# VectorE instead of GpSimd scales the softmax weights, and products, angle tiles, value projections and the opening's transposes change their places

## The chip, the cores and the metric

One core of one Trainium2 chip runs the whole layer. The metric is the device time of one execution in microseconds; lower is better. A group of runs is summed up by its median.

## The reference, cut to what matters

Four sequences of 512 tokens with 128 features pass an adaptive-layernorm block: an attention with 16 query heads, 4 key/value heads and 4 "nodes" per head, and a mixture of experts. The change lies in the attention alone:

```python
q, k, v = (x @ wq), (x @ wk), (x @ wv)              # heads of 64
logits = x @ wr                                     # 4 nodes for each token and head
tk_vals, tk_idx = top_k(logits, 2); tk_w = softmax(tk_vals)
pos = cumsum(member) - member                       # a token's place in each node's list
for n in range(4):
    c, s = cos_c[pos[..., n]], sin_c[pos[..., n]]   # rotary angles by that place
    qr = q * c + rotate_half(q) * s;  kr = k * c + rotate_half(k) * s
    scores = where(causal & member_of_n, qr @ kr.T * SCALE, NEG)
    outs[n] = softmax(scores) @ v
y = sum over the two chosen nodes of tk_w * outs[node]
x = x + gate * (y @ wo)                             # then the experts
```

## The kernel before

Each engine has its own instruction stream, written out in order; semaphores tie the streams together. After an opening (layernorm, ranking of the nodes, positions, the first rotary tables) one loop runs over k = 4n + s: n is one of 64 heads (4 sequences of 16), s one of 4 query tiles of 128 tokens, which sees (s+1)*128 keys. Each step works on two scores, one for each chosen node (e = 0, 1). After the loop come the experts, which the change leaves alone.

**A step, by engine.** TensorE (PE): `scores(k)`; `flip(k+2)`, the transposes of rotated q and k of a later step; `prob_rows(k-4)`, the transposes of weighted probabilities; in odd heads at s = 2 `values` (L1597), in heads with n % 4 = 2 at s = 2 `project_value`, in heads with n % 8 = 4 the output projection; at s = 3 `project(n+3)`. ScalarE (ACT): the copy of the flipped tile (`QK`, L740), the copy of the transposed probabilities (L751), `weigh_a(k-2)` (L772), which scales the first score's probabilities by its coefficient, then `exponentials(k)` (L763). VectorE (DVE): `row_max(k)` (L1147, L1157), `keep_angles` (L1069, L1071), `weigh_b(k-3)` (L1168, two inputs in SBUF beside the scalar), `inverse_sums(k-1)` (the reciprocal L1163), masks of the next head at s = 3 (L1141), `size_angles` (L1075), `products` (L1088). GpSimd (POOL): `rotate` in four parts for the head two ahead (L532 twice, L537, L540, L544, L548, L551), a split of expert weights at s = 1 of heads 2 to 49 (L571, L573), a split of later sequences' rows at s = 3 of heads 4 to 15 (L490, L492), and `coefficients(k-1)` (L560): `coef = rden * wslot` on 128x2.

**What sets the order.** A coefficient waits for its reciprocal; `weigh_a` and `weigh_b` wait for it. `rotate(m, 0)` waits for all four products of head m, which DVE makes in head m-2: two at s = 0 and two at s = 1. The last part of `rotate(m)` counts `k_done` up, and `flip(4m)`, which stands in PE's stream at s = 2 of head m-1 ahead of `values`, waits for it.

**PSUM.** Bank 7 (`psM`) holds in turn a head's projection, read by the products, the values, the value projection and the output projection. Banks 4 to 6 are a ring of turns (`turns`, `turn_bank`, `wait_turn`): flips, probability transposes and angle tiles take the next bank each, in PE's order, and wait for the reader of the turn three before. Banks 0 to 3 hold scores.

**Angle tiles.** Rotary tables are made for spans of 8 heads. The next span's four tiles stand in four heads one after the other (n % 8 = 0 to 3); at n % 8 = 4 ACT loads the sine table, makes sine and cosine of the span (L714, L715) and loads the exponential's table again (L808, L810).

**The opening.** `position_rows(b)` for the four sequences all use bank 4, so each waits for ACT's copy of the one before (`keep_positions`, L706); three of the four `chosen_rows` use bank 0 in the same way (L700). ACT loads the exponential's table (L726) ahead of those copies. The first flip waits for all four copies of positions and for the first head's rotation, which DVE makes (last line L1125).

## Time and profile before

| | us |
|---|---|
| median of 3 runs (918.26 to 919.42) | 919.1 |
| the profiled execution | 918.83 |
| its span, first to last instruction | 917.1 |
| loop, from the first to the last head's first score matmul | 58.87 to 783.8 |
| 8 heads in the middle (24 to 31) | 92.35 |

PE is busy 90% of the span, DVE 86%, ACT 80%, POOL 65%. The granted TensorE clock is 1.00 of full speed in the loop. From head 8 to head 55 eight heads take 92.2 to 92.6 us each time, so one such span stands for the rest. Matmuls overlap, so a busy PE is not a PE at its peak; an idle engine costs something only where the path runs through it.

### The profile page before, as it was taken

The numbers are of one execution on the slowest core, as the hardware profiler recorded it, in microseconds if no ns is written. First come the engines' busy times: TensorE is split into PE (matmuls) and PEld (weight loads), VectorE is DVE, ScalarE is ACT, GpSimd is POOL, SyncE is SP. The second block draws the span as 40 slices with busy tenths as digits, with TensorE's granted clock in tenths as the row PEclk, the third lists the DMA queues.
The fourth block names the chain that finished last, engine by engine and source line by source line (L and its number), as shares of the span: only waits on it lengthen the run. The fifth ranks groups of instructions, "written<-read, shape, count | busy, mean of one in ns | idle before, by whom it ended". The sixth has DMA issues, their size and how long they took to land. (4 is left out here: it accounts for less than half of the span.)

```text
span 917.1 us, 21368 instructions
## 1 busy us (share of the span) xinstructions
PE 826.5 (90%) x6552; PEld 580.4 (63%) x6552; DVE 792.9 (86%) x2003; ACT 733.0 (80%) x2001; POOL 600.4 (65%) x944
## 2 busy tenths in 40 slices
PE   4478989999999999999999999999999999999893
PEld 4456656666666666666666666666666666575793
DVE  6889978998899889988998899889988888777894
ACT  7268898889888988898889888988888887865572
POOL 4527768777877677767776777677656666127492
PEclk9699999999999999999999999999999999999997
DMA  9111111111211111111121111121101110323553
GB/s 219 32 18 30 37 31 43 37 36 25 43 41 37 24 41 39 38 29 37 36 41 30 39 37 36 32 41 31 14 9 16 16 14 13 127 70 93 153 166 113
DMA packets 81039, 45.01 MB, mean 49 GB/s; under 512 B 35072, under 2 KB 79808, under 8 KB 80928
## 3 DMA queue, kind: packets, MB, share of 16 engines
q1 hardware_dynamic: 79712, 41.15, 20.2%
q0 software_dynamic: 1216, 2.51, 0.8%
q8 instruction: 55, 0.90, 0.4%
q14 instruction: 56, 0.46, 0.2%
HBM read 30.62 MB, written 12.43 MB: 47 GB/s over the span
## 5 line engine op out<-in xcount | busy, mean ns | idle before, releaser
L1573 PE MATMUL psum<-QK 128*128 128x128 f32 (+3 forms) x1024 | 367.5, 451 | 2.3 <-ACT QK L740 1.8
L763 ACT ACTIVATE probs<-psum,negmax 128x128 f32<-128x128 f32 (+3 forms) x512 | 266.2, 527 | 48.6 <-DVE negmax L1157 32.5
L532 POOL TENSOR_TENSOR R<-pcs 128x512 f32<-128x512 f32 x126 | 172.7, 1392 | 59.7 <-DVE pcs L1088 59.7
L1573 PEld LDWEIGHTS psum<-QK 128*128 128x128 f32 x1024 | 158.3, 191 | 48.0 <-issue 41.8
L1168 DVE SCALAR_TENSOR_TENSOR accs<-probs,coef,accs 128x128 f32<-128x128 f32 (+3 forms) x256 | 164.7, 643 | 2.5 <-ACT accs L772 2.5
L772 ACT ACTIVATE accs<-probs,coef 128x128 f32<-128x128 f32 (+3 forms) x256 | 147.7, 577 | 23.4 <-POOL coef L560 23.2
L1088 DVE TENSOR_TENSOR pcs<-psum,arena 128x512 f32<-128x512 f32 x256 | 162.1, 674 | 1.7 <-POOL R L532 1.3
L560 POOL TENSOR_TENSOR coef<-rden,wslot 128x2 f32<-128x2 f32 x256 | 53.0, 207 | 167.9 <-DVE rden L1163 167.9
L1586 PE MATMUL psum<-ident,accs 128*128 128x128 f32 x640 | 115.9, 279 | 25.8 <-ACT QK L740 20.0
L1157 DVE CUSTOM_DVE_ANT_0 psum<-psum,outside 128x512 f32<-128x512 f32 x128 | 87.7, 700 | 51.4 <-PE psum L1575 50.7
L740 ACT ACTIVATE QK<-psum 128x384 f32<-128x384 f32 x235 | 115.6, 492 | 0.0
L1558 PE MATMUL psum<-ident,R 128*128 128x128 f32 x512 | 99.9, 277 | 11.0 <-issue 9.2
L751 ACT ACTIVATE arena<-psum 128x384 f32<-128x384 f32 (+1 forms) x242 | 107.0, 443 | 0.0
L1586 PEld LDWEIGHTS psum<-ident,accs 128*128 128x128 f32 x640 | 72.8, 140 | 51.2 <-issue 27.5
L1577 PE MATMUL psum<-mring 128*128 128x128 f16 (+2 forms) x384 | 104.8, 273 | 0.0
L763 ACT ACTIVATION_READ_ACCUMULATOR probs<-psum,negmax 128x1 f32 x512 | 103.1, 201 | 0.0
L1558 PEld LDWEIGHTS psum<-ident,R 128*128 128x128 f32 x512 | 56.6, 142 | 57.8 <-issue 51.4
L1147 DVE TENSOR_REDUCE negmax<-psum 128x2 f32<-128x256 f32 (+1 forms) x128 | 70.3, 550 | 18.9 <-PE psum L1577 18.0
L1575 PE MATMUL psum<-causal,identbig 128*128 128x128 f16 x384 | 84.3, 219 | 0.0
L1597 PE MATMUL psum<-arena,v_b 128*64 128x256 f32 (+3 forms) x512 | 76.0, 439 | 0.7 <-ACT arena L751 0.7
L1560 PE MATMUL psum<-ident,ktoks 128*128 128x128 f32 x256 | 69.9, 273 | 0.0
L1157 DVE CUSTOM_DVE_ANT_0 psum<-psum,causal 128x384 f32<-128x384 f32 x128 | 68.4, 573 | 0.6 <-PE psum L1577 0.6
(278 smaller groups left out, 1560.9 us busy)
## 6 DMA issues: line engine op xcount, KB each, us to landing
weight_halves<-whl SPq DMA_DIRECT2D x48, 128.0 KB, 2.2
arena<-weight_halves SPq DMA_DIRECT2D x22, 256.0 KB, 3.1
wrow<-words SPq DMA_DIRECT2D x64, 86.0 KB
arena<-weight_halves SPq DMA_DIRECT2D x7, 512.0 KB, 6.8
wrow<-words SPq DMA_DIRECT2D x64, 42.0 KB
wst<-in_L_ffn_w_up_dram SPq DMA_DIRECT2D x14, 128.0 KB, 2.4
wst<-in_L_ffn_w_gate_dram SPq DMA_DIRECT2D x14, 128.0 KB, 2.4
wst<-in_L_ffn_w_down_dram SPq DMA_DIRECT2D x14, 128.0 KB, 2.4
```

The lines of the kernel that those rows point to most:

```text
L532: pool.tensor_tensor(R[u][:, :, :, 0:3:2, half * HALF:(half + 1) * HALF].rearrange("p t e j f -> p (t e) j f"), halves(pc, half), halves(p ...
L740: act.activation(QK[:, n % 2, :, tb * P:(tb + 1) * P], turn_bank(("t", i))[:, 0:3 * P].rearrange("p (j t) -> p j t", j=3), ACT.Copy, scale ...
L751: act.activation(accT[:, n % 3, 0:w, ib * P:(ib + 1) * P], turn_bank(("pt", k))[:, 0:w * P].rearrange("p (j i) -> p j i", j=w), ACT.Copy). ...
L763: act.activation((expB if e else expA)[:, k % (4 if e else 3), 0:w], area, ACT.Exp, scale=1.0 if k % TB < 2 else -1.0, bias=negmax[k % 4][ ...
L772: act.activation(acc[k % 4][:, 0:w], expA[:, k % 3, 0:w], ACT.Copy, scale=coef[k % 4][:, 0:1]).then_inc(S["wa_done"], 1)
L1088: dve.tensor_tensor(dst[:, :, e, :].rearrange("p t (j f) -> p t j f", f=HALF), src, table.unsqueeze(2).to_broadcast([P, TB, 4, HALF]), ALU ...
L1157: dve.tensor_tensor_reduce(score_area(k, e), score_area(k, e), outside[:, e, 0:w].bitcast(BF16) if s == TB - 1 else causal[:, T - w:T], -1 ...
L1168: dve.scalar_tensor_tensor(acc[k % 4][:, 0:w], expB[:, k % 4, 0:w], coef[k % 4][:, 1:2], acc[k % 4][:, 0:w], ALU.mult, ALU.add).then_inc(S ...
L1558: pe.transpose(psT[:, e * P:(e + 1) * P], R[u][:, tb, e, 0:2, :].rearrange("p c d -> p (c d)"), ident[:, :])
L1573: pe.matmul(o, QK[:, u, e, rows], QK[:, u, 2, 0:w], start=True, stop=False)
L1577: mm_ = pe.matmul(o, mring[:, r, 1 + e, rows], mring[:, r, 0, 0:w], start=False, stop=True)
L1586: mm_ = pe.transpose(psPT[:, jb * P:(jb + 1) * P], acc[k % 4][:, jb * P:(jb + 1) * P], ident[:, :])
```

## The change

- `coefficients(k-1)` moves from POOL's stream to the end of DVE's step k, behind that step's products.
- The four products of head n+2 are no longer made as 2, 2, 0, 0 over the steps of head n: where n is even and n % 8 is not 4 they are made as 1, 2, 1, 0 (head 0 has an order of its own).
- Angle tiles 0 to 3 stay in heads 0 to 3; the others stand in odd heads from 5 to 51, one in each. `keep_angles` waits for the products that still read the table it overwrites.
- `project_value` goes to a turn bank, a new kind "v" in the ring, and waits for its turn instead of for the products. `project` no longer waits for `keep_value`.
- In the opening `position_rows` use banks 4, 4, 6, 5 and `chosen_rows` banks 0 to 3, with waits for the angles' readers; the table load of the exponential moves behind the first `keep_qk`; the second projection moves behind the transposes; one multiplication of the mixing weights (`dif * L`) moves from DVE to POOL.

```diff
 def angle_tile(k):
     n, s = k // TB, k % TB
-    if s == 1 and n % SPAN < TB and n // SPAN + 1 < NH // SPAN:
-        return n // SPAN * TB + n % SPAN
-    return None
+    if s != 1 or n >= (NH // SPAN - 2) * SPAN + TB:
+        return None
+    if n < TB:
+        return n
+    return n // SPAN * TB + (n % SPAN - 1) // 2 + 2 if n % 2 and n >= SPAN - 3 else None
+
+def products_at(k):
+    n, s = k // TB, k % TB
+    if n + 2 >= NH:
+        return ()
+    if n == 0:
+        return (((1, 2), (1, 3)), (), [(2, which) for which in range(4)], ())[s]
+    spread = n % 2 == 0 and n % SPAN != TB
+    of = (((0,), (1, 2), (3,), ()) if spread else ((0, 1), (2, 3), (), ()))[s]
+    return [(n + 2, which) for which in of]
...
+    if k % TB == 2 and k // TB % GROUP == 2 and k // TB // GROUP + 1 < B * KV:
+        turns.append(("v", k // TB // GROUP + 1))
...
 # GpSimd
-def coefficients(k):
...
+pool.wait_ge(S["lg_ev"], 2)
+pool.wait_ge(S["w_step"], 1)
+pool.tensor_tensor(dif, dif, L, ALU.mult).then_inc(S["w_step"], 1)
...
     if m < NH:
         rotate(m, part)
-    if k >= 1:
-        coefficients(k - 1)
 # ScalarE
 trigonometry(0)
-act.preload_act_table(ACT.Exp)
 keep_chosen(0, 0)
-keep_positions(1)
 keep_chosen(1, 0)
-keep_positions(2)
+for b in range(1, B):
+    keep_positions(b)
 keep_chosen(0, 1)
-keep_positions(3)
 keep_chosen(1, 1)
...
 keep_qk(0)
+act.preload_act_table(ACT.Exp)
 # VectorE
-dve.tensor_tensor(dif, dif, L, ALU.mult).then_inc(S["w_step"], 1)
...
+    if a >= TB:
+        dve.wait_ge(S["prod_done"], 4 * SPAN * (a // TB))
...
+def coefficients(k):
+    n, s = k // TB, k % TB
+    a = (n // H * TB + s) * H + n % H
+    if k == 0:
+        dve.wait_ge(S["w_done"], 2)
+    dve.wait_ge(S["rden_done"], k + 1)
+    dve.tensor_tensor(coef[k % 4][:, :], rden[k % 4][:, :], wslot[:, a, :], ALU.mult).then_inc(S["coef_done"], 1)
...
-    if k == 0:
-        products(1, 1)
-    elif n == 0 and s < 3:
-        products(2, s - 1)
-    elif s < 2 and n + 2 < NH:
-        products(n + 2, s)
+    for m, which in products_at(k):
+        product(m, which)
+    if 1 <= k <= STEPS:
+        coefficients(k - 1)
 # TensorE
 def position_rows(b):
     if b:
-        pe.wait_ge(S["row_ev"], b)
-    dst = bank[4]
+        pe.wait_ge(S["row_ev"], 1)
+    if b == 2:
+        pe.wait_ge(S["trig_done"], TB)
+        pe.wait_ge(S["ang_abs"], TB)
+    if b == 3:
+        pe.wait_ge(S["words_done"], 1)
+    dst = position_bank(b)                 # bank[(4, 4, 6, 5)[b]]
...
     if s == 2 and n % GROUP == 2 and n // GROUP + 1 < B * KV:
-        pe.wait_ge(S["prod_done"], 4 * (n + 3))
+        wait_turn(pe, ("v", n // GROUP + 1))
         project_value(n // GROUP + 1)
...
-        pe.wait_ge(S["v_ev"], min(B * KV, (n + 2) // GROUP + 1))
```

## Rows read from the trace of the kernel before

**Rows 1.** The page, part 1: busy time, share of the span, instructions.

```profile
PE 826.5 (90%) x6552; PEld 580.4 (63%) x6552; DVE 792.9 (86%) x2003; ACT 733.0 (80%) x2001; POOL 600.4 (65%) x944
```

**Rows 2.** Stretches of two heads, 24 to 31: length; busy by engine; clock; DMA.

```profile
339.08:361.66 22.58, 21.44 (x147) 14.08 (x145) 21.48 (x55) 18.84 (x58) 16.22 (x27) 1.00 0.18 37
361.66:384.25 22.59, 21.65 (x160) 14.50 (x157) 21.21 (x55) 19.12 (x59) 16.22 (x27) 1.00 0.18 37
384.25:409.82 25.57, 24.22 (x175) 17.20 (x173) 21.71 (x56) 23.11 (x57) 16.82 (x27) 1.00 0.17 33
409.82:431.43 21.61, 20.95 (x156) 14.15 (x153) 18.64 (x49) 18.92 (x59) 17.02 (x27) 1.00 0.19 39
```

**Rows 3.** The waits: engine, line, who released it; total, times, longest.

```profile
POOL coef L560 <- DVE rden L1163: 167.9, 156, 4.3
...
ACT accs L772 <- POOL coef L560: 23.2, 26, 4.5
```

**Rows 4.** Groups of DVE by line and shape: busy, mean ns, idle before.

```profile
L1088 DVE TENSOR_TENSOR pcs<-psum,arena 128x512 f32<-128x512 f32 x256 | 162.1, 674 | 1.7 <-POOL R L532 1.3 <-ACT arena L715 0.4
...
L1168 DVE SCALAR_TENSOR_TENSOR accs<-probs,coef,accs 128x128 f32<-128x128 f32 x64 | 32.5, 508 | 0.0
```

**Rows 5.** Timeline of DVE, heads 29 to 31: start, length, what, idle before.

```profile
409.20 0.35 DVE L1168 SCALAR_TENSOR_TENSOR accs<-probs,coef,accs 128x128 f32<-128x128 f32 x1
...
417.19 0.15 DVE L1163 RECIPROCAL rden<-den 128x2 f32<-128x2 f32 x1
...
418.69 1.01 DVE L1168 SCALAR_TENSOR_TENSOR accs<-probs,coef,accs 128x128 f32<-128x128 f32 x1
...
429.21 0.70 DVE L1157 CUSTOM_DVE_ANT_0 psum<-psum,outside 128x512 f32<-128x512 f32 x1 [2.09 <-PE psum L1575]
```

**Rows 6.** Timeline of POOL, heads 30 and 31.

```profile
415.45 2.94 POOL L532 TENSOR_TENSOR R<-pcs 128x512 f32<-128x512 f32 x2 [0.59 <-DVE pcs L1088]
...
418.51 1.04 POOL L537 TENSOR_TENSOR R<-R,code 128x512 f32<-128x512 f32 x1
...
421.46 0.19 POOL L560 TENSOR_TENSOR coef<-rden,wslot 128x2 f32<-128x2 f32 x1 [0.44 <-DVE rden L1163]
...
423.40 1.08 POOL L551 TENSOR_TENSOR ktoks<-R,kwork 128x256 f32<-128x256 f32 x1
```

**Rows 7.** Timeline of PE: the flip before head 31's values, head 32's first score.

```profile
424.94 0.38 PE L1558 MATMUL psum<-ident,R 128*128 128x128 f32 x2
...
431.43 0.44 PE L1573 MATMUL psum<-QK 128*128 128x128 f32 x2
```

**Rows 8.** Timeline of DVE in the opening: the first head's last rotation line.

```profile
55.92 0.42 DVE L1125 TENSOR_TENSOR ktoks<-R,kwork 128x256 f32<-128x256 f32 x1
```

**Rows 9.** Timeline of PE: the first flip; head 1's second score.

```profile
57.74 0.44 PE L1558 MATMUL psum<-ident,R 128*128 128x128 f32 x2 [0.24 <-ACT posT L706]
...
74.89 0.70 PE L1573 MATMUL psum<-QK 128*128 128x256 f32 x2 [1.37 <-ACT QK L740]
```

**Rows 10.** Timeline of ACT: table load, first exponential, the first two weighings.

```profile
49.51 1.28 ACT L726 ACT_TABLE_LOAD   x1
...
60.43 0.37 ACT L763 ACTIVATE probs<-psum,negmax 128x128 f32<-128x128 f32 x1 [1.22 <-DVE negmax L1147]
...
68.68 0.40 ACT L772 ACTIVATE accs<-probs,coef 128x128 f32<-128x128 f32 x1 [4.53 <-POOL coef L560]
...
72.62 0.51 ACT L772 ACTIVATE accs<-probs,coef 128x256 f32<-128x256 f32 x1 [2.04 <-POOL coef L560]
```

**Rows 11.** Timeline of POOL: head 1's rotation, with nothing between its parts.

```profile
61.73 2.50 POOL L532 TENSOR_TENSOR R<-pcs 128x512 f32<-128x512 f32 x2 [16.87 <-DVE pcs L1088]
...
67.58 0.72 POOL L551 TENSOR_TENSOR ktoks<-R,kwork 128x256 f32<-128x256 f32 x1
```

**Rows 12.** Stretches of two heads, 6 and 7, and 58 and 59.

```profile
132.22:154.02 21.80, 20.95 (x155) 14.15 (x153) 18.41 (x49) 19.01 (x59) 18.29 (x31) 1.00 0.19 39
...
729.91:751.47 21.56, 20.88 (x155) 14.22 (x153) 18.54 (x49) 18.91 (x59) 14.49 (x23) 1.00 0.11 15
```

More of the change, by code:

```diff
@@ L312, in turn_bank, with position_bank, value_bank @@
             return bank[4 + turn_of[what] % 3]
+        def position_bank(b):
+            return bank[(4, 4, 6, 5)[b]]
+        def value_bank(g):
+            return turn_bank(("v", g)) if g else psM
         def wait_turn(eng, what):
@@ L573, in split @@
                 pool.tensor_tensor(whl[:, 1, :], wst[:, :], whl[:, 0, :], ALU.subtract).then_inc(S["w_lo"], 1)
-            for k in range(STEPS + 1):
+            for k in range(STEPS):
                 n, s = k // TB, k % TB
@@ L700, in keep_chosen @@
                 act.activation(mk[0:HD, half * 2:half * 2 + 2, 1 + e, :],
-                               bank16[(0, 0, 5, 0)[e + 2 * half]][0:HD, 0:2 * NEAR].rearrange("p (b t) -> p b t", b=2), ACT.Copy,
+                               bank16[e + 2 * half][0:HD, 0:2 * NEAR].rearrange("p (b t) -> p b t", b=2), ACT.Copy,
                                scale=BIG).then_inc(S["mk_ev"], 1)
@@ L705, in keep_positions @@
                 act.wait_ge(S["row_mm"], b + 1)
-                act.activation(posT[0:PIECED, b * T:(b + 1) * T], bank[4][0:PIECED, :], ACT.Copy, scale=1.0 / TURN
+                act.activation(posT[0:PIECED, b * T:(b + 1) * T], position_bank(b)[0:PIECED, :], ACT.Copy, scale=1.0 / TURN
                                ).then_inc(S["row_ev"], 1)
@@ L1077, in size_angles, with product @@
                                   ).then_inc(S["ang_abs"], 1)
-            def products(n, e):
-                dve.wait_ge(S["qk_mm"], n + 1)
-                dve.wait_ge(S["trig_done"], TB + 1 + 2 * (n // SPAN))
-                if n >= 1 and e == 0:
-                    dve.wait_ge(S["add_done"], 2 * n)
-                src = psM.rearrange("p (t j f) -> p t j f", t=TB, f=HALF)
-                for i, dst in ((1, pc), (0, ps)):
-                    table = trig[:, n // SPAN % 2, i, n % SPAN, :, e, :]
-                    dve.tensor_tensor(dst[:, :, e, :].rearrange("p t (j f) -> p t j f", f=HALF), src,
-                                      table.unsqueeze(2).to_broadcast([P, TB, 4, HALF]), ALU.mult
-                                      ).then_inc(S["prod_done"], 1)
+            def product(n, which):
+                e, (i, dst) = which // 2, ((1, pc), (0, ps))[which % 2]
+                if which == 0:
+                    dve.wait_ge(S["qk_mm"], n + 1)
+                    dve.wait_ge(S["trig_done"], TB + 1 + 2 * (n // SPAN))
+                    if n >= 1:
+                        dve.wait_ge(S["add_done"], 2 * n)
+                src = psM.rearrange("p (t j f) -> p t j f", t=TB, f=HALF)
+                table = trig[:, n // SPAN % 2, i, n % SPAN, :, e, :]
+                dve.tensor_tensor(dst[:, :, e, :].rearrange("p t (j f) -> p t j f", f=HALF), src,
+                                  table.unsqueeze(2).to_broadcast([P, TB, 4, HALF]), ALU.mult
+                                  ).then_inc(S["prod_done"], 1)
             def first_rotation():
@@ L1100, in over_slot @@
                     return t_.unsqueeze(2).to_broadcast([P, TB, HD])
-                for e in range(2):
-                    products(0, e)
+                for which in range(4):
+                    product(0, which)
                 dve.wait_ge(S["code_e"], 2)
@@ L1129, in _ @@
             dve.tensor_reduce(lmax[:, 0, :], dif, AX_X, ALU.add).then_inc(S["w_step"], 1)
-            products(1, 0)
+            for which in range(2):
+                product(1, which)
             dve.tensor_scalar(shift[:, :, :, :].rearrange("p b h s -> p b (h s)"),
@@ L1438, in project_value @@
                 for tb in range(TB):
-                    mm_ = three(psM[:, tb * HD:(tb + 1) * HD], rows_of(b, tb),
+                    mm_ = three(value_bank(g)[:, tb * HD:(tb + 1) * HD], rows_of(b, tb),
                                 [w_v[:, l, (g % KV) * HD:(g % KV + 1) * HD] for l in range(2)], True, True)
@@ L1473, in chosen_rows @@
                 pe.wait_ge(S["sel_cp"], e + 1)
-                if half and not e:
-                    pe.wait_ge(S["words_done"], 1)
-                else:
-                    pe.wait_ge(S["mk_ev"], 4 + e + half)
+                pe.wait_ge(S["mk_ev"], 4)
+                if e + half:
+                    pe.wait_ge(S["trig_done"], TB)
+                    pe.wait_ge(S["ang_abs"], TB)
                 for t_ in range(B // 2 * (TB - 1)):
                     tile = (half * B // 2 + t_ // (TB - 1)) * TB + t_ % (TB - 1)
-                    mm_ = pe.transpose(bank16[(0, 0, 5, 0)[e + 2 * half]][0:HD, t_ * P:(t_ + 1) * P], sel16[:, e, tile * 64:(tile + 1) * 64],
+                    mm_ = pe.transpose(bank16[e + 2 * half][0:HD, t_ * P:(t_ + 1) * P], sel16[:, e, tile * 64:(tile + 1) * 64],
                                        ident16[:, :])
```

22 lines of the change are left out of this document (8 added, 14 removed).

## The prediction

> **What bounds the kernel now.** I read the page's busy shares first [rows 1], then the stretches of two heads in the loop [rows 2], then the waits [rows 3], then the timelines. No engine is full over the whole span, but in the loop the two heads 24/25 and 26/27, which hold two angle tiles each, have DVE busy for 21.48 of 22.58 us and 21.21 of 22.59: 95% and 94% [rows 2]. There DVE sets the pace. The pair 30/31 has no tile, takes 21.61 us, and DVE works 18.64 of it; it waits 2.09 us for scores behind the values [rows 2, 5]. The pair 28/29 takes 25.57 because of the tables and the output projection [rows 2]. So eight heads cost 92.35 us, and DVE is busy 83.04 of them, about 90%. POOL's 167.9 us of waiting for reciprocals [rows 3] is idle time of an engine that does not bind; ACT's 23.2 us of waiting for coefficients [rows 3] can matter.
>
> **Part 1, the coefficients go to DVE.** The sum needs the price of a DVE operation on 128x2 with two inputs in SBUF, which the trace lacks. The nearest row is the reciprocal on 128x2, 0.15 us long, whose successor starts about 0.08 after it [rows 5]: 0.1 us of DVE's line, my estimate, times 256. But there is more. `weigh_b` on 128x128 takes 0.35 us when POOL is idle; at 418.69 it took 1.01, while POOL's L537 ran from 418.51 to 419.55 [rows 5, 6]. It ended 0.15 us behind POOL's instruction, as if it had waited for it and then run. Over all 64 of that shape the mean is 508 ns [rows 4], 0.16 more than the free one. It goes both ways: two L532 that a `weigh_b` comes between take 2.94 us, two that ran free 2.50 [rows 6, 11]. A coefficient also reads two SBUF tensors, and POOL is busy 66.28 of 92.35 us [rows 2]. I take 0.15 us of waiting per coefficient, by the 508 ns row; the bounds are 0 and 0.66 (1.01 less 0.35).
>
> The Trainium skill states a rule that speaks against this part: page "SBUF — State Buffer", section "Who interferes with whom", says that a VectorE instruction with two SBUF inputs and a GpSimd instruction that reads SBUF exclude each other, and whoever issues second blocks until the first is done. The rows just named agree. By that rule, if coefficients mostly arrive second, the time would be near the slow rival's 943 us; without it near the fast rival's 912, both worked out below from rows.
>
> In eight heads DVE gets 32 coefficients: 3.2 us of work and 4.8 of waiting, 83.0 to 86.2 or 91.0. At the 95% that the busiest pair reaches, eight heads then need 90.7 or 95.8 us, against 92.35. So this part alone allows anything from a gain of 1.7 to a loss of 3.4 in each span, and the detail decides.
>
> **Part 2, products 1, 2, 1 and angle tiles in odd heads.** Moving a tile costs no work. With two tiles a pair has 2.6 to 2.8 us more DVE work than without [rows 2], some 1.4 each, and the 2.09 us of waiting in an odd head [rows 5] hides one. That is the gain: the two angle pairs lose a tile in their even head. The pair 30/31, and 28/29, gain a tile instead.
>
> The price lies in POOL. In head 30 POOL starts the rotation at 415.45, as the second pair of products ends, and ends it at 424.48 (423.40 + 1.08): 9.03 us [rows 6]. PE's flip of that head starts at 424.94, 0.46 later, at once behind its scores [rows 7]. Now the fourth product follows the third reciprocal (417.19) instead: 417.19 + 0.08 + 0.67 [rows 5, 4] is 417.9, less 0.3 that a lighter first step saves (my estimate): 417.6, against 415.4. POOL's 9.03 us shrink: three coefficients leave it (0.19 each) and the 0.44 us wait for a reciprocal [rows 6]: 8.0, and I take 8.1, with one of DVE's coefficients in between. If both L532 run free, as at 61.73 [rows 11], 7.7; if DVE's coefficients come between its parts as `weigh_b` does, 8.6. So the rotation ends at 417.6 + 0.1 + 8.1 = 425.8, and the flip, which could start at 424.6, waits for it. Behind that flip stand in PE's stream the probability transposes, `values`, the next scores and the next head: from the flip to head 32's first score PE needs 6.49 us [rows 7] without a pause. The pair therefore takes 21.61 + 425.8 - 424.94 = 22.5 us (22.1 by 7.7, 23.0 by 8.6). The three pairs of a span that are spread have the same structure afterwards, so all three get 22.5, against 22.58, 22.59 and 21.61: +0.7 in a span, +0.24 a pair.
>
> - Spread pairs among heads 16 to 49: 13, +3.1 us.
> - Heads 6 to 15 also split rows on POOL, 18.29 us a pair against 17.02 [rows 12, 2], some 0.6 a head in the same chain: 23.0 for four pairs, two of which stood at 21.8 [rows 12] and two near 22.6: +3.1. Head 2 keeps its tile and spreads too, so its fourth product comes 1.4 us later still: +0.9, an estimate.
> - Pairs with tables, seven: the step before the sine tables stays 2, 2, 0, 0 and gets two coefficients of 0.25 us ahead of ACT's chain; I take +0.4 each, +2.8 (0 to +1).
> - After head 49 POOL has no weight split and the chain is a microsecond shorter, so flips do not wait: four pairs, one of which loses its even tile, three at 21.56 [rows 12]: -1.0 in all.
>
> **Part 3, values in a turn bank.** It lets the value projection run before the spread product; its turn's reader, ACT's copy, is done by then. The next flips find their bank a turn later. I cost it at nothing, covered by PE's score matmuls of s = 3; if uncovered, about 0.15 us in 15 heads, inside the range.
>
> **Part 4, the opening.** The first flip starts at 57.74, released by ACT's positions copy [rows 9]; the rotation that it also needs ends at 56.34 (55.92 + 0.42) [rows 8]. With more banks the copies are early, so it gains up to 1.3 us. The table load of 1.28 us now stands before the second copy and the first exponential, which had waited 1.22 us idle [rows 10]; that hides most of it, 0.3 stays: -1.0 (bounds 0 and -1.3). Then the first two coefficients: ACT waited 4.53 and 2.04 us for them behind POOL's rotation [rows 10]. On DVE the first is ready before ACT comes; the second stands behind four products at once. Head 1's second score at 74.89, held by ACT's copy [rows 9], can come 1.7 us earlier (bounds 0 and 2.5); its rotation on POOL, 61.73 to 68.30 [rows 11], is not shortened. The multiplication that leaves DVE costs nothing either way: DVE waits for the angles behind it, and POOL, which takes it, is idle until 61.73 (16.87 us, rows 11). Sum: -2.7.
>
> **The sum.** -2.7 + 0.9 + 3.1 + 3.1 + 2.8 - 1.0 = +6.2 us on the profiled execution's 918.8 (917.1 span and 1.7 around it; the median of the runs is 0.3 higher): **925.0 us**, slower by 0.7%.
>
> **Rivals.**
> - *Faster: POOL's chain is short enough.* If coefficients slip between POOL's instructions and the chain takes 7.6 us, the flip waits for nothing that ACT's copy does not hold too, and spread pairs run at 21.9: 13 x -0.36 is -4.7, the early four +1.1, head 2 +0.3, tables +1.4, the end -1.4, the opening -3.5: -6.8, 912 us. It decides where the rotation ends less than 0.3 us behind the old flip. For it: DVE's 18.64 us in the pair 30/31 leave room, and the coefficients of even heads' first three steps meet an idle POOL. Against it: two L532 at 2.94 us and a slack of 0.46 us.
> - *Slower by much: DVE becomes the bound.* If coefficients wait for POOL as the 418.69 row did, DVE's 91.0 us per span at 95% make 95.8, spread pairs 23.1: +10.9, early four +5.9, head 2 +1.5, tables +7, the end +1, the opening -2: +24, 943 us.
> - *No change: gains and losses cancel.* Pairs at 22.26, their mean now, 0; early four +2, head 2 +0.5, tables +1.4, the end -1, the opening -2.9: 918.8. Then the spread only trades DVE's wait for POOL's.
>
> **How the numbers follow.** A measurement of this kernel can tell about 0.2%, 1.8 us. Chances: forecast 0.42, its own range 921 to 932; faster rival 0.32; no change 0.13; slow rival 0.13. So faster 0.32, same 0.13, slower 0.55. Eight in ten lie between 909 and 938: the lower end leaves the outer third of the faster rival, the upper half of the slow one.
>
> **What would show it.** Right: DVE's share in the loop rises above 93%; groups of the coefficient show a mean well over 0.15 us; PE's flip (the transposes of R) shows idle time before it in odd heads, released by POOL's last rotation line; spread pairs at about 22.5 us. ACT's long waits for coefficients in heads 0 and 1 are gone, and the first score comes near 57.9. Wrong: coefficients at 0.15 us flat, flips without idle time, or pairs below 22.0; then the first rival holds. Pairs above 23 with DVE over 96% busy speak for the second.

## The result: 941.5 us, slower by 2.5%

| | before | changed |
|---|---|---|
| median of 4 runs, us | 919.26 (918.26 to 920.74) | 941.54 (939.83 to 945.22) |
| the profiled execution, us | 918.83 | 941.49 |
| ratio, 95% interval | | 1.0246 (1.0213 to 1.0280) |

The page of the changed kernel, part 1, to be read beside [rows 1]:

```profile
PE 830.0 (88%) x6552; PEld 585.5 (62%) x6552; DVE 868.8 (92%) x2258; ACT 739.3 (79%) x2001; POOL 565.4 (60%) x689
```

The stretches of two heads, 24 to 31, and their sum, beside [rows 2]:

```profile
352.47:375.31 22.84, 21.07 (x146) 14.01 (x143) 22.80 (x60) 19.16 (x60) 15.83 (x19) 1.00 0.21 36
375.31:398.08 22.77, 20.99 (x158) 14.35 (x155) 22.73 (x60) 18.92 (x59) 15.06 (x19) 1.00 0.20 36
398.08:424.78 26.70, 24.76 (x178) 17.46 (x175) 25.52 (x67) 23.49 (x59) 15.35 (x19) 1.00 0.16 32
424.78:447.82 23.04, 21.22 (x158) 14.37 (x155) 23.00 (x60) 19.16 (x61) 15.33 (x19) 1.00 0.18 37
sum 95.35, PE 88.04 PEld 60.18 DVE 94.06 ACT 80.73 POOL 61.57; mean PE 22.01 PEld 15.05 DVE 23.52 ACT 20.18 POOL 15.39
```

The third number of work in a row is DVE's: 94.06 of 95.35 us, against 83.04 of 92.35 before. In the pairs without tables DVE has 0.04 us to spare. So eight heads cost 3.0 us more, and DVE's time grew by 11.0. The waits, beside [rows 3]:

```profile
POOL R L554 <- DVE pcs L1101: 253.3, 54, 13.5
...
ACT accs L784 <- DVE coef L1185: 52.3, 134, 2.3
...
PE psum L1583 <- POOL ktoks L573: 12.0, 9, 1.7
```

ACT waits twice as long for coefficients as before (52.3 against 23.2 us). The flips (L1583) do wait for POOL's last rotation line, as forecast, but for 12.0 us in all. The groups of DVE by shape, beside [rows 4]:

```profile
L1185 DVE TENSOR_TENSOR coef<-rden,wslot 128x2 f32<-128x2 f32 x256 | 73.4, 287 | 0.5
...
L1190 DVE SCALAR_TENSOR_TENSOR accs<-probs,coef,accs 128x128 f32<-128x128 f32 x64 | 40.0, 625 | 0.0
...
L1087 DVE TENSOR_SCALAR arena<-arena 128x512 uint32<-128x512 uint32 x28 | 29.1, 1041 | 0.0
...
L1061 DVE TENSOR_SCALAR arena<-psum 128x512 uint32<-128x512 uint32 x4 | 2.8, 692 | 1.4 <-PE psum L1555 1.4
```

The coefficient is there with 0.287 us in the mean, and `weigh_b` on 128x128 went from 508 to 625 ns. The surprise is L1087, the sign line of an angle tile (`size_angles`). Before, the same group reads:

```profile
L1075 DVE TENSOR_SCALAR arena<-arena 128x512 uint32<-128x512 uint32 x28 | 11.4, 407 | 0.0
```

Nobody touched its work, and it costs 17.7 us more. The timelines of DVE, then of POOL, in head 29 of the changed kernel show how:

```profile
421.45 0.15 DVE L1177 RECIPROCAL rden<-den 128x2 f32<-128x2 f32 x1
421.52 1.19 DVE L1087 TENSOR_SCALAR arena<-arena 128x512 uint32<-128x512 uint32 x1
422.64 0.68 DVE L1185 TENSOR_TENSOR coef<-rden,wslot 128x2 f32<-128x2 f32 x1
```

```profile
421.05 1.38 POOL L559 TENSOR_TENSOR R<-R,code 128x512 f32<-128x512 f32 x1
422.39 0.90 POOL L562 TENSOR_TENSOR kwork<-R 128x256 f32<-128x256 f32 x1
```

L559 runs until 422.43, and the sign line ends 0.28 after it; L562 runs until 423.29, and the coefficient, 0.14 us when free, ends 0.03 after it. Each DVE line stands behind a POOL line that was there first. It is so with the other sign lines: one of the 28 meets no POOL line and takes 0.41 us; the other 27 take from 0.43 to 1.42 us, 20 of them 1.19 to 1.20, and each ends 0.28 to 0.29 us behind the POOL line that had begun before it.

### The profile page after: what moved, and what is told of

Read it like the earlier page. It is cut to its first block and busy times, and to the rows that moved or that the text cites. A ratio compares the mean times of both kernels' runs of the same rounds, so it can differ in the third digit from the quotient of the medians.

```text
span 939.7 us, 21282 instructions
## 1 busy us (share of the span) xinstructions
PE 830.0 (88%) x6552; PEld 585.5 (62%) x6552; DVE 868.8 (92%) x2258; ACT 739.3 (79%) x2001; POOL 565.4 (60%) x689
## 5 line engine op out<-in xcount | busy, mean ns | idle before, releaser
L554 POOL TENSOR_TENSOR R<-pcs 128x512 f32<-128x512 f32 x126 | 165.9, 1337 | 253.6 <-DVE pcs L1101 253.3
L784 ACT ACTIVATE accs<-probs,coef 128x128 f32<-128x128 f32 (+3 forms) x256 | 145.5, 568 | 52.8 <-DVE coef L1185 52.3
L1190 DVE SCALAR_TENSOR_TENSOR accs<-probs,coef,accs 128x128 f32<-128x128 f32 (+3 forms) x256 | 174.7, 682 | 1.7 <-ACT accs L784 1.7
L1583 PE MATMUL psum<-ident,R 128*128 128x128 f32 x512 | 100.7, 279 | 23.9 <-POOL ktoks L573 12.0
L1583 PEld LDWEIGHTS psum<-ident,R 128*128 128x128 f32 x512 | 58.5, 143 | 69.3 <-issue 66.8
L559 POOL TENSOR_TENSOR R<-R,code 128x512 f32<-128x512 f32 x63 | 73.1, 1161 | 4.1
L1185 DVE TENSOR_TENSOR coef<-rden,wslot 128x2 f32<-128x2 f32 x256 | 73.4, 287 | 0.5
```

The source lines that it names most:

```text
L554: pool.tensor_tensor(R[u][:, :, :, 0:3:2, half * HALF:(half + 1) * HALF].rearrange("p t e j f -> p (t e) j f"), halves(pc, half), halves(p ...
L784: act.activation(acc[k % 4][:, 0:w], expA[:, k % 3, 0:w], ACT.Copy, scale=coef[k % 4][:, 0:1]).then_inc(S["wa_done"], 1)
L1190: dve.scalar_tensor_tensor(acc[k % 4][:, 0:w], expB[:, k % 4, 0:w], coef[k % 4][:, 1:2], acc[k % 4][:, 0:w], ALU.mult, ALU.add).then_inc(S ...
L1583: pe.transpose(psT[:, e * P:(e + 1) * P], R[u][:, tb, e, 0:2, :].rearrange("p c d -> p (c d)"), ident[:, :])
```

## The experiments

Ratios are against the kernel before, on the same chip; its median lay between 918.7 and 920.8 us on the chips used, so two times of this table can differ by some 2 us for that alone. "Eight heads" are heads 24 to 31, with DVE's busy time behind the slash.

| kernel | us | ratio (95%) | eight heads / DVE |
|---|---|---|---|
| before | 919.3 | | 92.35 / 83.04 |
| changed | 941.5 | 1.0246 (1.0213 to 1.0280) | 95.35 / 94.06 |
| 1 coefficients alone | 964.7 | 1.0491 (1.0459 to 1.0523) | 99.30 / 95.58 |
| 2 changed, coefficients back | 978.2 | 1.0632 (1.0599 to 1.0665) | 98.90 / 83.80 |
| 3 changed, tiles back | 958.2 | 1.0402 (1.0367 to 1.0437) | 97.57 / 93.24 |
| 4 opening and values alone | 930.3 | 1.0111 (1.0088 to 1.0135) | 93.37 / 82.74 |
| 5 changed, sign line late | 941.3 | 1.0232 (1.0188 to 1.0276) | 94.72 / 90.63 |
| 6 changed, scalar coefficients | 947.8 | 1.0310 (1.0265 to 1.0355) | not used |
| 7 both of 5 and 6 | 953.7 | 1.0359 (1.0322 to 1.0397) | not used |
| 8 opening alone | 921.4 | 1.0015 (0.9994 to 1.0036) | not used |
| 9 changed, split behind | 928.9 | 1.0091 (1.0057 to 1.0126) | 93.39 / 91.48 |
| 10 both of 5 and 9 | 929.6 | 1.0111 (1.0073 to 1.0150) | 93.26 / 90.62 |
| 11 as 10, coefficients early | 963.0 | 1.0461 (1.0425 to 1.0497) | not used |
| 12 opening, tiles, values | 919.4 | 0.9986 (0.9968 to 1.0004) | 91.78 / 83.94 |
| 13 changed, products two and two | 950.8 | 1.0318 (1.0270 to 1.0365) | 96.39 / 95.00 |
| 14 tiles and values alone | 918.9 | 0.9988 (0.9970 to 1.0006) | not used |
| 15 as 14, split behind | 919.0 | 0.9980 (0.9959 to 1.0000) | not used |
| 16 as 14, early heads mended | 915.8 | 0.9959 (0.9945 to 0.9974) | 91.75 / 83.91 |

### 1. The coefficients alone

```diff
 # before, POOL
-    coefficients(k - 1)
 # before, DVE, behind products
+    coefficients(k - 1)
```

> The kernel before with one change: the 256 coefficients stand on VectorE, behind the products of their step, and no longer on POOL. Opening, products (2, 2, 0, 0), angle tiles and values stay. In the changed kernel DVE is busy 94.06 of 95.35 us in heads 24 to 31, against 83.04 of 92.35 before; coefficients are 9.4 us of that, weigh_b 3.0 more, the sign line of the angle tiles 3.2 more. Theory (DVE is the bound, and the coefficients make it so): this part alone does most of the loss. DVE's work for eight heads goes to 92 to 98 us, the span of eight heads to 94 to 97, and, with no gain from the opening, the time to 932 to 945. Rival (the forecast's: the late fourth product makes POOL's rotation late and flips wait): nothing is late here, POOL loses 6.6 us of coefficients in eight heads, DVE's 3.2 us of work goes into its idle time, and the time is 916 to 923. Also open: does the sign line, 0.40 us before and 1.19 in the changed kernel, lengthen here too, where the tiles stand as before? If POOL's waits for reciprocals kept its long lines out of its way, yes (over 0.7); if it was the place in odd heads, no (0.40).

Measured: 964.7, worse than the changed kernel. Its first two pairs of the eight heads, and the sum:

```profile
350.71:375.64 24.93, 21.65 (x147) 14.05 (x145) 24.86 (x62) 18.93 (x57) 15.69 (x19) 1.00 0.16 33
375.64:400.83 25.19, 22.05 (x159) 14.52 (x157) 25.12 (x63) 19.64 (x61) 15.48 (x19) 1.00 0.16 33
...
sum 99.30, PE 89.09 PEld 60.17 DVE 95.58 ACT 81.93 POOL 61.83; mean PE 22.27 PEld 15.04 DVE 23.90 ACT 20.48 POOL 15.46
```

DVE is full in the pairs with two tiles (24.86 of 24.93), and the sign line is long here too, with the tiles where they always stood:

```profile
L1064 DVE TENSOR_SCALAR arena<-arena 128x512 uint32<-128x512 uint32 x28 | 28.9, 1033 | 0.0
```

So its length comes from the coefficients' move and not from the odd heads. The size was missed: even the theory said 945 at most for the time and 97 for eight heads.

### 2. The changed kernel with the coefficients back on POOL

```diff
 # changed, DVE
-    coefficients(k - 1)
 # changed, POOL, behind rotate
+    coefficients(k - 1)
```

> The changed kernel with the coefficients back on POOL, at the end of each of its steps as before; opening, spread products, angle tiles in odd heads and values in a turn bank stay. Theory (DVE is the bound through the coefficients, their waiting for POOL, and what POOL's free run does to weigh_b and the sign line): DVE falls back to some 83 to 85 of 92 us in eight heads, the sign line goes back to 0.40 to 0.6 us, and the time is 912 to 921. Rival 1 (POOL's late rotation is what costs): with coefficients between its lines the rotation is longer still, 9.0 us instead of 8.0 from the fourth product on, flips wait over 1.5 us in 13 pairs, and the time is 930 to 945. Rival 2 (the sign line is blocked because of its place in odd heads, whoever makes the coefficients): its mean stays near 1.19 us, and the time lies between, 921 to 928.

Measured: 978.2, outside every expectation, with DVE at ease (83.80 of 98.90). The sign line is short again, although it stands in odd heads. Timelines of DVE, then of POOL, in head 25:

```profile
384.00 0.40 DVE L1098 TENSOR_SCALAR arena<-arena 128x512 uint32<-128x512 uint32 x1
```

```profile
384.16 0.30 POOL L582 TENSOR_TENSOR coef<-rden,wslot 128x2 f32<-128x2 f32 x1 [0.71 <-DVE rden L1188]
384.42 1.04 POOL L559 TENSOR_TENSOR R<-R,code 128x512 f32<-128x512 f32 x1
```

That is the mechanism. POOL's coefficient waits for DVE's reciprocal (0.71 us idle), the sign line starts right behind that reciprocal, and L559, the line that would block it, can't start before the coefficient. POOL's waiting kept its long lines out of DVE's way. Without coefficients nothing holds POOL back.

What makes this kernel slow is another thing, the spread products: without them (run 12) it takes 919.4. Timelines of POOL, ACT and PE in heads 24 and 25:

```profile
371.25 2.58 POOL L554 TENSOR_TENSOR R<-pcs 128x512 f32<-128x512 f32 x2 [2.91 <-DVE pcs L1112]
373.78 0.20 POOL L582 TENSOR_TENSOR coef<-rden,wslot 128x2 f32<-128x2 f32 x1
```

```profile
374.07 0.51 ACT L795 ACTIVATE accs<-probs,coef 128x256 f32<-128x256 f32 x1 [2.57 <-POOL coef L582]
```

```profile
376.44 0.30 PE L1612 MATMUL psum<-ident,accs 128*128 128x128 f32 x1 [2.77 <-ACT QK L763]
```

POOL waits 2.91 us for the fourth product, runs two rotation lines, and only then the coefficient that ACT and PE need. So the spread is to be had only with the coefficients off POOL.

### 3. The changed kernel with the angle tiles back

The four tiles of eight heads stand in heads 24 to 27 again.

> The changed kernel with the angle tiles back where they stood, in heads 24 to 27 of each eight (even and odd), all else as changed. Theory (DVE is the bound; the sign line is long only where POOL's rotation runs): the tiles of even heads meet an idle POOL, so half of the sign lines return to 0.40, 2 x 0.79 = 1.6 us of DVE in eight heads; the pairs with two tiles grow to 24 and over, the pairs without fall below 22.5, and the sum falls by 1 to 2 us in eight heads: 932 to 940. Rival (the tiles' balance is what keeps the odd heads' flips on time): two tiles in a pair push products and with them POOL's rotation later, the sum of eight heads grows, and the time is 943 to 950.

Measured: 958.2. The sign lines are shorter (0.74 us in the mean), yet the sum for eight heads is larger, since the pairs with two tiles are full and the others can't fill up. The theory's 932 to 940 is wrong, and the rival, right in direction, said 950 at most; evening out the tiles is worth 16.7 us to the changed kernel, though the values' bank, run 4, has a part in that.

### 4 and 8. The opening, with and without the values' turn bank

Run 4 is the kernel before with the new opening and values in a turn bank; run 8 keeps the values in bank 7.

> The kernel before with the opening of the changed one (five banks for the positions and chosen rows, the multiplication on POOL, the table load behind the first keep_qk, head 2's products at one step) and values in a turn bank; coefficients on POOL, products (2, 2, 0, 0) and angle tiles as before. Every theory expects the loop of heads 16 to 49 as before, 92.3 us for eight heads. The first score stands at 56.5 in the changed kernel against 58.9 before: if that gain of 2.4 us is kept, the time is 916 to 917.5. If ACT's waits for the first coefficients (4.5 and 2.0 us) take it back, 918 to 920.

> The kernel before with the new opening alone; the values' projection goes back to the bank of the projections, as before. The run with both the opening and the values in a turn bank took 930.3: there PE's value projection of head 26 waited 1.70 us for DVE to read the angle tile that has the bank, and the pair 26/27 took 23.6 us against 22.6; six pairs of that kind lost 1.0 to 2.7 us each. Theory (values in a turn bank cost that much where an angle tile stands in the same head, and the opening itself gains or loses little): 918 to 922. Rival 1 (the opening is what costs, through heads 0 and 1, 27.4 us there against 24.4): 922 to 926. Rival 2 (neither; the late heads lose it): 928 to 931.

Measured: 930.3, above both expectations of run 4, and 921.4, as run 8's theory said. The values' bank costs 8.9 us where tiles stand in the same head. Timeline of PE in run 4, head 26, the value projection:

```profile
377.37 0.20 PE L1448 MATMUL psum<-w_v,hT 128*128 128x64 f16 x1 [1.70 <-DVE arena L1092]
```

It waits 1.70 us for DVE to read the angle tile that has its bank. Against run 8 the pairs with such a head take 1.0 to 2.7 us more. The opening alone is no gain that can be told. From the first rotation line to the first score run 8 needs 5.8 us against 6.9 before, but heads 0 and 1 then take 27.4 us instead of 24.4; ACT waits 4.50 us for the first coefficient, as before [rows 10].

### 5, 9 and 10. The sign line late; the split behind the rotation; both

```diff
 # 5, changed, DVE: three steps later
-if k >= 1 and angle_tile(k - 1) is not None:
-    size_angles(angle_tile(k - 1))
+if k >= 4 and angle_tile(k - 4) is not None:
+    size_angles(angle_tile(k - 4))
 # 9, changed, POOL
-if s == 1 and 0 <= n - RING < UNITS * PIECES:
-    split(n - RING)
 ...
 rotate(m, part)
+if s == 1 and 0 <= n - RING < UNITS * PIECES:
+    split(n - RING)
```

> The changed kernel with the sign line of an angle tile (0.40 us on VectorE when POOL is idle, 1.19 in 22 of 28 cases of the changed kernel) moved three steps later, into the next head's second step, where POOL has ended its rotation; nothing else differs. Theory (DVE is full, and the sign line waits for POOL's R lines, which no longer stop for reciprocals): the mean falls from 1.04 to 0.40, 28 x 0.64 = 18 us of DVE's line go, 3.0 us in eight heads, and as DVE is busy 98.6% there the time falls by 10 to 18 us, to 923 to 932. Rival 1 (the wait only moves on: what stands behind the sign line, the coefficient of that step, then meets the same R line and blocks in its place): the sign line shortens, the coefficients lengthen by as much, and the time is 938 to 942. Rival 2 (flips that wait for POOL's rotation set the pace, as the forecast had it): no change, 940 to 943.

> The changed kernel with one move on POOL: the weight split of a head (two lines, 1.15 us) stands behind the last part of the rotation instead of ahead of it. In the changed kernel it ran at 423.94 between two rotation lines, and the flip of that pair waited 1.1 us for the rotation's last line. Theory A (DVE's full line sets the pace, 94.06 of 95.35 us in eight heads): flips no longer wait, but the pairs stay, and the time is 936 to 942. Theory B (the forecast's: POOL's rotation and the flip behind it set the pace of spread pairs): each spread pair loses up to 1.1 us, 13 or more of them, and the time is 922 to 931.

> The changed kernel with both moves: the sign line three steps later (with that alone DVE had 4.1 us of idle time in eight heads instead of 1.3, the pairs went to 22.70 and no lower, and three flips in eight heads waited 1.0 to 1.1 us for POOL's last rotation line), and the weight split behind the rotation. Theory C (two limits lie side by side, DVE's line and POOL's rotation, and an edit to one alone shows nothing): now the pairs fall to 21.7 to 22.3, eight heads to 91.5 to 93.5, and the time to 925 to 935. Theory D (the third limit is ACT, which waits for coefficients 4.8 us in eight heads as they stand behind the products): pairs stay at 22.5 to 22.8 and the time at 938 to 942.

Run 5: the sign line is back at 0.437 us, DVE's time in eight heads falls by 3.4 us, and the time stays (941.3). Its sum, its waits for POOL, and the timeline of PE at one of those flips:

```profile
sum 94.72, PE 87.97 PEld 59.98 DVE 90.63 ACT 80.70 POOL 61.35; mean PE 21.99 PEld 14.99 DVE 22.66 ACT 20.17 POOL 15.34
```

```profile
PE psum L1583 <- POOL ktoks L573: 20.0, 17, 1.7
```

```profile
390.40 0.41 PE L1583 MATMUL psum<-ident,R 128*128 128x128 f32 x2 [1.01 <-POOL ktoks L573]
```

The flips' waits grew from 12.0 to 20.0 us: behind DVE stood the forecast's own limit. In heads 24 to 31 three flips wait for POOL where one did, and the three spread pairs take 22.70 to 22.71 us. Run 9 shortens that chain by the split's 1.15 us and gives back 12.6 us, with DVE still at 98%:

```profile
368.34:390.71 22.37, 21.29 (x158) 14.35 (x155) 22.02 (x60) 19.09 (x59) 15.50 (x19) 1.00 0.18 37
...
417.33:439.39 22.06, 21.29 (x157) 14.35 (x155) 21.73 (x58) 18.77 (x59) 15.28 (x18) 1.00 0.19 39
sum 93.39, PE 88.37 PEld 60.16 DVE 91.48 ACT 80.45 POOL 61.89; mean PE 22.09 PEld 15.04 DVE 22.87 ACT 20.11 POOL 15.47
```

```profile
PE psum L1583 <- POOL ktoks L573: 1.9, 3, 0.8
```

Two things went at once. The flips wait 1.9 us instead of 12.0. And `weigh_b` lost 8.7 us (174.7 to 166.0 in the page), since it now meets other POOL lines. The 128x128 line in the last step of head 30 of the changed kernel, and of head 26 of run 9 (where it starts between two lines of POOL), on timelines of DVE:

```profile
434.12 1.39 DVE L1190 SCALAR_TENSOR_TENSOR accs<-probs,coef,accs 128x128 f32<-128x128 f32 x1
```

```profile
377.71 0.35 DVE L1190 SCALAR_TENSOR_TENSOR accs<-probs,coef,accs 128x128 f32<-128x128 f32 x1
```

No run separates the two, but the traces do in part. In the pairs 26/27 and 30/31 no flip of the changed kernel waits for POOL, and yet run 9 makes them 0.40 and 0.98 us shorter, as `weigh_b` puts 1.0 and 1.3 us less on DVE's line there. The eight spread pairs of that kind among heads 16 to 49 give 5.6 of the 12.1 us that the heads up to 61 gain. In the pairs 6/7 to 10/11 it is the other way round: `weigh_b` costs 2.2 us more, the flips wait 3.1 us less, and the pairs gain 2.1. Run 10 adds the late sign line and gains nothing more (929.6): DVE then has 2.6 us of idle time in eight heads, the flips wait 2.5 us for POOL in all, none of it in these heads, and what holds eight heads at 93.26 us is open.

### 6, 7 and 11. Coefficients without a second tensor, and early

```diff
 # 6, changed, DVE
-dve.tensor_tensor(coef[k % 4][:, :], rden[k % 4][:, :], wslot[:, a, :], ALU.mult)
+dve.tensor_scalar(coef[k % 4][:, 0:1], rden[k % 4][:, 0:1], wslot[:, a, 0:1], None, ALU.mult)
+dve.tensor_scalar(coef[k % 4][:, 1:2], rden[k % 4][:, 1:2], wslot[:, a, 1:2], None, ALU.mult)   # then_inc as before
 # 11: as 10, and coefficients(k - 1) directly behind inverse_sums(k - 1)
```

> The changed kernel with each coefficient line (128x2, two tensor inputs) replaced by two lines of 128x1, whose second factor is a scalar of each partition and no tensor input; same place, same result. In the changed kernel a coefficient takes 0.145 us when it is free and 0.287 in the mean, up to 1.04, and puts 6.98 us on DVE's line in eight heads, 0.22 each, of which some 0.07 each is what a free one puts there. Theory (the rest is waiting for POOL at a shared port that only a second tensor input needs): the new lines take 0.14 to 0.16 us whatever POOL does, two of them put 0.15 to 0.2 us on the line, ACT's 52 us of waiting for coefficients shrinks, and the time falls by 2 to 10 us, to 931 to 939. Rival 1 (it is not the second input; any line that reads SBUF beside POOL waits): the new lines are as long as the old, twice as many, and the time is 948 to 960. Rival 2 (the waiting moves into weigh_b, which comes after): lines short, weigh_b longer, 940 to 943.

> Both of the two other edits in the changed kernel: the sign line three steps later, and coefficients as two 128x1 lines with a scalar factor. Theory: 3.0 us of blocked sign lines and 0.5 to 2.5 of blocked coefficients leave DVE's line in eight heads; DVE then has 88 to 90 us of work there, the rotation and the flips, or PE with 88 us, come next, eight heads take 91 to 93 us, and the time is 914 to 925, so that it may come below the kernel before (919). Rival (the waits for POOL move on to the next line with two inputs, and DVE's full state stays): 935 to 942.

> As the run before this one, and the coefficient line stands directly behind the reciprocal of its step, ahead of the products, so that ACT's weighing need not wait for two products of 0.67 us. Theory C (DVE's line and POOL's rotation are the limits): within 4 us of the run before it. Theory D (ACT's waits, 52 us in the whole changed kernel, are a limit of their own): ACT's waits fall below 15 us, and the time is 5 to 15 us below the run before. Rival (early, the coefficient meets POOL's lines more often than behind the products): its mean goes from 0.29 us to over 0.4, and the time goes up.

Run 6, groups of DVE:

```profile
L1185 DVE TENSOR_SCALAR coef<-rden,wslot 128x1 f32<-128x1 f32 x256 | 51.6, 202 | 0.5
L1186 DVE TENSOR_SCALAR coef<-rden,wslot 128x1 f32<-128x1 f32 x256 | 51.4, 201 | 0.0
```

Shortest 195, longest 217 ns in 512 lines: without the second tensor input none of these lines waits for POOL. But each takes 0.20 us and not the 0.15 that was expected, so the pair is no cheaper than a coefficient that waits now and then (0.287): in eight heads it puts 8.2 us on DVE's line instead of 7.0. The theory's 931 to 939 is wrong; rival 1's time nearly fits (947.8), its reason does not. Eight heads take 95.36 us, as in the changed kernel. The kernel loses 6.3 us; of the 4.8 us between the profiled executions 4.6 come in heads 50 to 61, and why is open. Run 7 loses more (953.7), outside the theory and the rival, and its cause is open too. In run 11 ACT's waits for coefficients fall from 38.6 us (run 10) to 5.4, as the theory said, yet the coefficient's mean rises to 0.427 us and the time to 963.0. In eight heads the coefficients put 12.2 us on DVE's line instead of 8.1, and the eight heads take 97.33 us instead of 93.26: the rival is right, early it meets POOL more often.

### 12 and 13. Which part loses

Run 12 is the changed kernel with coefficients on POOL and products two and two; run 13 has products two and two and keeps the coefficients on DVE (`spread = False`).

> The changed kernel without the coefficients' move and without the spread products: coefficients on POOL and products (2, 2, 0, 0) as before, but the new opening, angle tiles in odd heads, values in a turn bank. Before, the pairs with two tiles took 22.58 us at 95% of DVE and the pair without 21.61. Theory (DVE's uneven load is what the loop before lost, and one tile in each pair evens it; the values' projection finds its bank free, as no tile stands in its head): pairs at 21.9 to 22.2, eight heads 91.0 to 92.0 instead of 92.35, the time 914 to 919. Rival (the odd head's tile delays products, rotation and flip of a head that had 0.46 us of slack): 92.5 to 95 for eight heads, 921 to 932.

> The changed kernel with products (2, 2, 0, 0) in all heads, as before; coefficients on VectorE, angle tiles in odd heads, opening and values as changed. Theory B (the fourth product, one step later, makes POOL's rotation and the flip behind it late, which is the forecast's mechanism): the rotation begins some 2.5 us earlier in spread pairs, flips do not wait, the three pairs fall from 22.8 to 21.9 to 22.3, and the time is 924 to 932. Rival (VectorE's load sets the pace: the same work in fewer steps packs two products ahead of two coefficients and makes it worse): pairs at 23 to 24.5, the time 945 to 960, as the run with the coefficients alone (pairs with tiles at 25) suggests.

With runs 2, 12 and 13 there is a square, all with the new opening, tiles and values:

| | products 2, 2, 0, 0 | products 1, 2, 1, 0 |
|---|---|---|
| coefficients on POOL | 919.4 | 978.2 |
| coefficients on DVE | 950.8 | 941.5 |

So the coefficients' move costs 31.4 us, and the spread, which is bad without it, gives 9.3 of them back. Run 13 has its rotation early, no flip in it waits for POOL, and it is slower, as the rival said, with DVE at 95.00 of 96.39:

```profile
sum 96.39, PE 89.87 PEld 60.15 DVE 95.00 ACT 81.87 POOL 62.04; mean PE 22.47 PEld 15.04 DVE 23.75 ACT 20.47 POOL 15.51
```

The late fourth product is therefore not what the change mainly loses by. In run 12 one tile in each pair helps by itself, 91.78 us for eight heads instead of 92.35; heads 0 to 5 take it back, and the time ends just above the 914 to 919 of the theory.

### 14, 15 and 16. A version below both

Run 14 is the kernel before with only the tiles and the values' bank changed, run 15 adds the split's move. Run 16 mends run 14's early heads:

```diff
 # 16, against 14
-    return n // SPAN * TB + (n % SPAN - 1) // 2 + 2 if n % 2 and n >= SPAN - 3 else None
+    if n <= SPAN + TB:
+        return {7: 4, 8: 5, 9: 6, 11: 7}.get(n)
+    return n // SPAN * TB + (n % SPAN - 1) // 2 + 2 if n % 2 else None
...
-    return turn_bank(("v", g)) if g else psM
+    return turn_bank(("v", g)) if g > 1 else psM
...
```

> The kernel before with angle tiles in odd heads and values in a turn bank; opening, products and coefficients as before. The same with the new opening took 919.4, with pairs at 21.95 in the loop (91.78 us for eight heads against 92.35), but 27.5 us in heads 0 and 1 against 24.4. Theory (the new opening, with coefficients on POOL, loses in heads 0 and 1 what it gains up to the first score, since the first coefficients and rotations on POOL come no earlier): within 2 us of that run, 918 to 920.5. Rival (the 3.0 us of heads 0 and 1 are a loss of their own, head 2's products at one step): 914.5 to 917.

> As the run before this one, and the weight split stands behind POOL's last rotation part. Theory (with products two and two, the rotation ends long before its flip is due, also where a split stands in it; the flips of that kernel wait for nothing on POOL): within 1.5 us of the run before this one. Rival (the split delays lines of POOL that VectorE's weigh_b then waits for at the shared port, whatever the products do): 3 to 8 us below it.

> The kernel before with one angle tile in each pair of heads and values in a turn bank (opening, products and coefficients as before), like the run with the old opening, 918.9, but head 2, which has a tile of its own, projects its values into the bank of the projections as before, and the second group's tiles stand in heads 7, 8, 9 and 11 instead of 5, 7, 9 and 11, out of the heads with the first tables. Theory (these two are what heads 2 to 5 lose: 24.4 and 27.1 us against 23.4 and 25.6): the pairs 2/3 and 4/5 go back to 23.4 and 25.6, the pair 8/9 takes 22.6 instead of 22.1, and the time is 915.5 to 917.5, below both kernels. Rival (the time of those heads comes from the order of POOL's and ACT's work there, whatever the tile and the values do): 918 to 920.

Runs 14 and 15, 918.9 and 919.0, can't be told from before, or from run 12; the split limits nothing where POOL is paced by coefficients. Run 16 takes 915.8, 0.4% below the kernel before. Its eight heads:

```profile
337.88:359.83 21.95, 20.91 (x145) 13.93 (x143) 20.24 (x52) 18.64 (x58) 16.73 (x27) 1.00 0.18 37
...
sum 91.75, PE 88.61 PEld 59.96 DVE 83.91 ACT 79.57 POOL 66.41; mean PE 22.15 PEld 14.99 DVE 20.98 ACT 19.89 POOL 16.60
```

The pair 2/3 went back to 23.4 us, as expected; the pair 4/5 did not (26.7, not 25.6). Its row:

```profile
104.91:131.65 26.74, 24.11 (x144) 15.00 (x141) 20.62 (x54) 23.12 (x57) 18.18 (x31) 0.87 0.16 32
```

DVE and ACT do the work of before (20.61 and 23.12 us there), but the granted clock is 0.87 instead of 1.00, and PE is busy 24.11 us instead of 21.46. So this run can't tell what the tile in head 5 costs: the clock hides it.

## Why the prediction was wrong

The direction was right, the time (941.5) lies above the range. By the groups of the sum, from the first scores of the heads in both traces:

| term | forecast | measured |
|---|---|---|
| opening, heads 0 and 1 | -2.7 | -1.8 |
| pair 2/3 | +0.9 | +4.4 |
| four early pairs | +3.1 | +3.6 |
| 13 spread pairs | +3.1 | +7.5 |
| seven table pairs | +2.8 | +9.0 |
| late pairs | -1.0 | -0.9 |
| from head 62 on | 0 | +0.8 |
| sum | +6.2 | +22.6 |

- **The step that failed** is in part 2: there the length of a spread pair, 22.5 us, was taken from POOL's chain and PE's flip alone, while part 1's own count, DVE at 90.7 to 95.8 us for eight heads, was left as "anything". In the loop DVE's line was the longer of the two: 94.06 us of work in 95.35, the spread pairs at 22.77 to 23.04 us with 0.04 us of DVE idle in each, and one flip in eight heads that waits for POOL. Runs 1 and 13 show it: with the rotation early, the loss is larger. Of the 16.4 us between forecast and measurement the spread pairs are 4.4, the table pairs 6.2 and the pair 2/3 3.5.
- **Luck.** The slow rival (943, chance 0.13) had the mechanism. That its time is so near is luck: the 95.8 us behind it are 91.0 us of DVE work at 95%, and the trace shows 94.06 at 98.6%; its spread pairs (+10.9 against +7.5) and its pair 2/3 (+1.5 against +4.4) miss in opposite directions.
- **The coefficient's price** was right. Forecast 0.25 us, measured 0.287. From the start of each to the start of the next line, idle time taken off, 32 of them put 7.0 us on DVE's line in eight heads; forecast 8.0.
- **What the sum lacked** are two DVE lines that nobody moved. Counted in the same way, the sign line adds 3.0 us in eight heads (four lines of 1.19 instead of 0.40; by run 1 through the coefficients' move) and `weigh_b` 2.3. I priced what DVE gets, and not what POOL, freed of 167.9 us of waiting [rows 3], would do to DVE's other lines. I called that waiting idle time of an engine that doesn't bind. It was what kept POOL in step with DVE (run 2).
- **The rule on ports** was read for one line and not for the rest. The section that the prediction names, "Who interferes with whom" of the Trainium skill's "SBUF — State Buffer", also says that `tensor_scalar` can run in a mode that takes the shared port pair, and that GpSimd and such a line then shut each other out. The trace agrees: the sign line takes 0.40 us from SBUF when it waits for nothing, 0.69 from PSUM (L1061), and mostly 1.19 beside POOL's rotation.
- **POOL's chain**: the flips do wait for it, 12.0 us in all, and 20.0 when DVE is relieved (run 5). The spread pairs of run 5, at 22.7 us, are near the forecast's 22.5. As a second limit its mechanism is real and about rightly sized; it stood close behind the first.
- **Table pairs** were forecast at +0.4 and took +1.1 in the loop. Run 12, with coefficients on POOL and a tile in head 29, already takes 25.91 instead of 25.57, run 1, with coefficients on DVE and no tile there, 26.37: some 0.3 for the tile and 0.8 for the coefficients. The first of them, 4/5, took +3.3.
- **Heads 2 to 5** lost 7.7 us. In the pair 2/3 (+4.4), which holds two tiles, most of it is the coefficients: run 1, which moves them alone, takes 27.40 us there instead of 23.36, with DVE busy 27.14. The clock is not needed for it: run 13 takes 27.19 at a granted clock of 1.00. The values' projection in head 2, which shares its head with a tile, costs 1.0 where the coefficients stay on POOL (runs 14 and 16). In the pair 4/5 (+3.3) a part is the clock: by run 16, where DVE and ACT have no more work than before, some 1.2 us (an estimate: 26.74 there against 25.58 before). The rest is open. In head 5 of the changed kernel PE waited twice, and the stretch from 126 to 132 had a granted clock of 0.50, the lower of its two levels (1.2 GHz); before, the heads 2 to 5 were granted 1.00 (the heads 0 and 1 0.93). A timeline of PE and that stretch of the changed kernel:

```profile
124.96 0.44 PE L1611 MATMUL psum<-ident,accs 128*128 128x128 f32 x2 [1.76 <-DVE accs L1190]
127.14 0.61 PE L1539 MATMUL psum<-turns_off,posT 96*128 96x512 f16 x1 [1.74 <-ACT arena L763]
```

```profile
126.00:132.00 6.00, 4.86 (x13) 2.91 (x14) 5.03 (x14) 4.57 (x17) 2.31 (x2) 0.50 0.00 0
```

- **The opening**: the step -1.0 up to the first score was right. From DVE's first rotation line to the first score the changed kernel needs 5.95 us, before 6.87. The other 1.5 us by which the first score is earlier lie ahead of that line and can't be credited to the change: with the old opening it starts at 49.74 in run 1, 51.14 in run 14 and 52.00 before. The step -1.7 for heads 0 and 1 was wrong: they took 0.6 us more (25.03 instead of 24.42). Run 8 shows that the new opening by itself makes them 3.0 us longer, run 1 that the coefficients alone make them 1.0 us shorter; the sum had only the gain.
- **Values in a turn bank** cost nothing where no tile stands in the head, as forecast; with one they cost 1.0 to 2.7 us a time (run 4), which the sum did not see for head 2.

## What to carry to other kernels

When work leaves an engine that waits much, ask what its waiting held back: here GpSimd's waits for VectorE's reciprocals were what kept its long lines from meeting VectorE's. Price a move for every line of the receiving engine that the engine set free can hold up, not only for the lines that move. Where two counts give two lengths for one stretch, the longer one is the forecast, and the shorter one is what appears next when the first is mended.

## What was not expected of the hardware

- A sign line on 128x512 in SBUF with a single tensor input took 0.40 us beside a waiting GpSimd and 1.19 beside a running one in 20 of 28 cases; wherever a GpSimd line had begun before it, it ended 0.28 to 0.29 us behind that line.
- A 128x1 line whose factor is a scalar of each partition took 0.195 to 0.217 us in 512 cases, more than a free 128x2 line with two tensor inputs (0.141 at the least), but never waited for GpSimd.
- An engine that is 98% busy by the page need not be the limit by that much: run 9 took 2.6 us in eight heads from VectorE's busy time without touching a line of it, because part of what counts as busy is waiting for GpSimd: `weigh_b` alone put 2.6 us less on its line.
